# A norm's bias made with one streamed input, and a side factor loaded earlier into another home

## Chip, cores and metric

The kernel runs on one core of a Trainium2 chip. The metric is the device time of one execution in microseconds (us), the median of three. The engines are TensorE (PE in the rows; PEld is its weight load), VectorE (DVE), ScalarE (ACT), GpSimd (POOL) and SyncE (SP; SPq is its queue, which issues all DMAs). They run their own instruction streams in order and meet at semaphores.

## The reference

Two transformer layers with sandwich norms over x of 2 x 512 tokens and 512 channels. Each of four parts has, in short, the form

```python
x = x + _layernorm(part(_layernorm(x, axis=-1), ...), axis=-1)
```

with `part` = causal grouped attention with rotary embedding (32 heads, 8 key heads); a linear layer with a side branch; full attention with normed queries and keys (32 heads); a gated feed-forward layer with side branches. The linear part is

```python
h = jnp.einsum('bsd,nrd->nbsr', x, lora_A)
coef = (SCALE * lora_weights)[:, None, None]
lora_out = jnp.einsum('nbsr,nor->bso', h, lora_B * coef)
base = jnp.einsum('bsd,od->bso', x, W) + bias
return base + lora_out
```

and the norm is (x - m) / sqrt(v + eps) over the last axis, for each token.

## The kernel before

A tile is 128 tokens (8 tiles, 4 to a batch). Products are made of three fp32r matmuls (L83 to L85), with each operand split into `hi` and `lo`: ScalarE copies `hi`, VectorE or GpSimd subtracts (`rest`, L90) to get `lo`.

**The norm of rows** (class RowNorms) takes one tile at a time over three engines. VectorE makes statistics (L133), mean and variance (L139) and variance plus eps (L142). GpSimd takes the root (`root`, L148: the power -0.5 into `rstd`). VectorE makes the bias -mean*rstd (`center`, L154), and ScalarE applies scale and bias to the tile (`scaled`, L160). Every `[128, 1]` value of this is one column of a small tensor. The names are `first_norm` (8 tiles, before the first attention), `lin_norm` (4 rounds of 8: attention's output, linear input, linear output, next input) and `ffn_norm` (3 rounds of 8): 64 biases in all.

**The opening** runs the first norm over the 8 tiles. In each round VectorE centers tile t, then makes `xT_lo` of tile t-2 (L90). GpSimd's stream has, from tile 3 on, one split of a weight (L90, `l_w_k_lo` and `l_w_q_lo`) behind each root. TensorE turns the tiles and puts the first key and query projections between them.

**The first attention** runs 8 passes (one per key head) of 32 steps. What an engine does at a step is fixed by tables (`USES0`, `OUTS0`, `LOADS0`, `FETCH0`). Softmax rows are turned by VectorE (L1543) into `l_blocks`, moved between partitions by 16 DMAs for each pair of heads (L1236, `l_moved<-l_blocks`), and the sum over keys (`pv`) is scaled by VectorE (L1494, `l_scaled`). A pair's move waits until the buffer's earlier pair has gone through L1494.

**The last pass** goes on past step 32 and overlaps with the linear part (class Linear), whose constants are steps of that pass. The side factors are merged into the weight: `la` (factor a) and `lb` (factor b times mix times 2) are split, TensorE multiplies them at step 34 and 36 (MERGE), VectorE adds the product to the weight (L987), ScalarE and GpSimd split that. The loads are SP's: `load_a` at 12 into `l_raw_k`, `load_w` at 22 into `l_raw_q`, `load_b` at 28 into `l_raw_v`, which also issues the 1 MB load of `x` into `l_rope`. Since `l_raw_v` lies on the low half of the value weight, `load_b` waits for the last value projection. At SIDE (31) VectorE multiplies factor b by the mix (L976). From step 39 on, the norms of the linear part run, one or two tiles a step. GpSimd adds residuals there (L1050 `add`, L1053 `add_out`) behind its roots.

**The feed-forward phase** begins with the norms of 8 tiles in the same way (L2009 is its residual addition on GpSimd), while weights are merged and split.

Of the kernel before, what the change touches and what calls it, by code (L numbers as in the profile page):

```python
# [17 lines left out]
ALU = mybir.AluOpType  # L18
ACT = mybir.ActivationFunctionType
# [68 lines left out]
def rest(engine, out, full, hi):  # L88

    return engine.tensor_tensor(out, full, hi.bitcast(F32), ALU.subtract)  # L90
# [27 lines left out]
class RowNorms:  # L118
# [32 lines left out]
    def center(self, dve, r, t):  # L151

        dve.wait_ge(self.rooted[r], t + 1)
        dve.scalar_tensor_tensor(self.bias[:, r, t:t + 1], self.mean_var[:, r, t, 0:1], -1.0,  # L154
                                 self.rstd[:, r, t:t + 1], ALU.mult, ALU.mult).then_inc(self.biased[r], 1)

# [641 lines left out]
class Linear:  # L798
# [8 lines left out]
    FIRST = [(GH - 1) * TB + TB * GH * b + OUT0_AT + 1 for b in range(B)]  # L807
    LOAD_A, LOAD_W, LOAD_B, LOAD_LATE, SIDE, MERGE = 12, 22, 28, 33, 31, 34
    END = FIRST[1] + TB + AT[1]["split_next"]

    def __init__(self, p, ctx, ctx0, home, banks, xT, acc, ident, half, x_rows, kept):
        sem = lambda n: p.sem(ctx0, f"lin_{n}")
        self.p, self.nc, self.a = p, p.nc, p.a
        self.xT, self.acc, self.ident, self.x_rows, self.kept = xT, acc, ident, x_rows, kept
        self.w, self.la, self.lb, self.w_words, self.a_words, self.b_words, self.z, self.rope, self.blocks, self.bias = home
        self.z_next = self.rope[:, 2]
        self.x_first = self.rope[:, 0:2].rearrange("p a b s -> p (a b) s")
        self.x = [self.x_first[:, t] for t in range(TB)]
        self.x_second = self.blocks[:, 0].rearrange("p g c e i -> p (g c e i)")[:, 0:TB * D]            .rearrange("p (t d) -> p t d", t=TB)
        self.x += [self.x_second[:, t] for t in range(TB)]  # L820
        self.mix = p.sb(ctx, "lin_mix", [8 * RK, 1])
        self.score, self.general, self.out_bank, self.spare, self.brief = banks
        self.norms = RowNorms(p, ctx, ctx0, "lin_norm", 4, half)
        self.s_x = [sem("x_in0"), sem("x_in1")]
        self.s_a, self.s_b, self.s_w = sem("a_in"), sem("b_in"), sem("w_in")
        self.s_hi, self.s_lo, self.s_merged, self.s_whole, self.s_w_hi, self.s_w_lo, self.s_rows, self.s_taken = map(
            sem, "hi lo merged whole w_hi w_lo rows taken".split())
        self.s_add, self.s_add_out, self.s_turn, self.s_x_hi, self.s_x_lo = map(
            sem, "add add_out turn x_hi x_lo".split())
        self.s_turn_next, self.s_next_hi, self.s_next_lo, self.s_kept = map(  # L830
            sem, "turn_next next_hi next_lo kept".split())
# [27 lines left out]

    def load_a(self, sp):  # L860
        sp.dma_start(self.a_words[:], self.a["l0_a"]).then_inc(self.s_a, 16)

    def load_w(self, sp):
        sp.dma_start(self.w_words[:], self.a["l0_w"].rearrange("(c p) o -> p c o", p=P)).then_inc(self.s_w, 16)

    def load_b(self, sp):
        sp.dma_start(self.b_words[:], self.a["l0_b"]).then_inc(self.s_b, 16)
        sp.dma_start(self.x_first, self.x_rows[:, 0:TB]).then_inc(self.s_x[0], 16)
# [79 lines left out]
    def scalar(self, act, n):  # L948
# [4 lines left out]
        if n == self.SIDE + 1:  # L953
            act.wait_ge(self.s_lo, 1)
            act.activation(self.lb.hi, self.b_words[:], ACT.Copy).then_inc(self.s_hi, 1)
        for c in {self.MERGE + 2: (0, 1), self.MERGE + 4: (2, 3)}.get(n, ()):
# [16 lines left out]
    def vector_weights(self, dve, n):  # L973
        if n == self.SIDE:
            dve.wait_ge(self.s_b, 9 * 16)
            dve.tensor_scalar(self.b_words[:], self.b_words[:], self.mix[:], 2.0, ALU.mult, ALU.mult).then_inc(self.s_lo, 1)  # L976
        if n == self.SIDE + 1:
            dve.wait_ge(self.s_hi, 1)
            rest(dve, self.la.lo, self.a_words[:], self.la.hi).then_inc(self.s_lo, 1)
        if n == self.SIDE + 2:  # L980
            dve.wait_ge(self.s_hi, 2)
            rest(dve, self.lb.lo, self.b_words[:], self.lb.hi).then_inc(self.s_lo, 1)
        for c in {self.MERGE + 1: (0, 1), self.MERGE + 3: (2, 3)}.get(n, ()):
# [84 lines left out]
def grouped_attention(p, ctx0, xT, acc, ident, half, x_rows, kept, inv_rows):  # L1068
# [4 lines left out]
    with ExitStack() as ctx:  # L1073
# [79 lines left out]

        home = w_q, w_k[:], w_v[:], raw_q, raw_k, raw_v, trig, rope, blocks, mask
        last_pass = Pass(NG - 1, False, True, Linear.END)
# [36 lines left out]
        def _(sp):  # L1192
# [49 lines left out]
            def body(m):  # L1242
                for n in m.steps():
# [3 lines left out]
                    if pair is not None:  # L1247
                        move(m, pair)
                    if m.last and n == Linear.LOAD_A:
                        sp.wait_ge(s_bank, m.done(USES0, ("k", 1)))  # L1250
                        linear.load_a(sp)
                    if m.last and n == Linear.LOAD_W:
                        sp.wait_ge(s_bank, m.done(USES0, ("q", SLOTS - 1)))
                        linear.load_w(sp)
                    if m.last and n == Linear.LOAD_B:
                        sp.wait_ge(s_bank, m.done(USES0, ("v", 1)))
                        sp.nop(nofuse=True)
                        sp.wait_ge(s_rope_lo, m.done(USES0, ("q", SLOTS - 1), 0, of_qk))
                        linear.load_b(sp)
                    if m.last and n == Linear.LOAD_LATE:  # L1260
# [851 lines left out]
```

## Time and profile before

| | |
|---|---|
| median of 3 runs | 2323.69 us (2321.89 to 2324.77) |
| the profiled execution, its own time | 2323.8 us |
| its span | 2321.4 us |
| TensorE busy | 2112.8 us (91%) |
| VectorE busy | 1686.7 us (73%) |
| ScalarE busy | 1351.7 us (58%) |
| GpSimd busy | 1237.5 us (53%) |
| mean granted TensorE clock | 0.954 |

Busy time is the sum over an engine's instructions. The granted clock is 1.0 at 2.4 GHz and 0.5 at 1.2 GHz. The profiled execution lies 0.1 us from the median, so that a sum made against it holds for the median too.

### The profile page before, as it was taken

What the parts mean: (1) busy time and instruction counts of PE and PEld (TensorE: products, weight loads), DVE (VectorE), ACT (ScalarE), POOL (GpSimd) and SP (SyncE); (2) the same over time, 40 slices, a digit from 0 to 9 for tenths busy, and PEclk for the clock granted to TensorE, in tenths of its full rate; (3) what the DMA queues carried; (4) which work ended last, traced back from release to release, by engine and by line L of the source; (5) the groups of instructions that cost most, each with busy time, mean ns of one, the idle gap of its engine ahead of it and who ended that gap; (6) DMA issues with size and microseconds to landing.
All of it is one profiled execution on the core that took longest, in us unless ns stands there. A gap on an engine that the chain in (4) does not pass through costs nothing. (4 is left out here: it accounts for less than half of the span.)

```text
span 2321.4 us, 38455 instructions
## 1 busy us (share of the span) xinstructions
PE 2112.8 (91%) x10535; PEld 1781.2 (77%) x10535; DVE 1686.7 (73%) x2961; ACT 1351.7 (58%) x3637; POOL 1237.5 (53%) x996
## 2 busy tenths in 40 slices
PE   4899999999998745999999999999999999857998
PEld 3688888888886634888888888888888888635887
DVE  4788888888887772787878788787887888864422
ACT  4777777777776333665665656656656666433321
POOL 4878777787784434544545545455444454323400
PEclk8999999999999867999999999999999999977999
DMA  2344444434435111444444444344444443442210
GB/s 78 103 117 111 112 109 115 120 97 119 120 93 149 54 48 48 108 119 111 108 99 119 104 115 106 95 112 110 115 107 104 102 116 89 107 117 89 79 46 28
DMA packets 165903, 231.96 MB, mean 100 GB/s; under 512 B 47280, under 2 KB 77136, under 8 KB 165744
## 3 DMA queue, kind: packets, MB, share of 16 engines
q1 hardware_dynamic: 165744, 229.97, 37.1%
q8 instruction: 83, 1.36, 0.3%
q14 instruction: 76, 0.62, 0.1%
HBM read 114.23 MB, written 6.55 MB: 52 GB/s over the span
## 5 line engine op out<-in xcount | busy, mean ns | idle before, releaser
L90 POOL TENSOR_TENSOR l_probsT_lo<-l_moved,l_probsT_hi 128x512 fp32r<-128x512 f32 (+2 forms) x256 | 281.7, 1105 | 315.9 <-ACT l_probsT_hi L579 286.2
L573 ACT ACTIVATE l_probs<-l_score,l_negtop 128x512 f32<-128x512 f32 x256 | 175.7, 686 | 384.4 <-DVE l_negtop L675 384.1
L90 DVE TENSOR_TENSOR l_probsT_lo<-l_moved,l_probsT_hi 128x512 fp32r<-128x512 f32 (+1 forms) x256 | 284.4, 1111 | 30.5 <-ACT l_probsT_hi L579 30.4
L675 DVE TENSOR_REDUCE l_negtop<-l_score 128x1 f32<-128x512 f32 x256 | 175.8, 687 | 102.6 <-PE l_score L85 100.8
L1435 ACT ACTIVATE l_probs<-l_score,l_negtop 128x128 f32<-128x128 f32 (+3 forms) x256 | 134.8, 527 | 176.9 <-DVE l_negtop L1524 175.4
L83 PE MATMUL l_score<-l_kT_lo,l_qT_hi 128*128 128x512 f32 (+3 forms) x512 | 191.6, 374 | 50.4 <-POOL l_qT_lo L90 27.8
L83 PE MATMUL l_general<-l_w_qk_lo,xT_hi 128*128 128x512 f32 x512 | 201.1, 393 | 28.5 <-POOL l_w_qk_lo L90 28.5
L83 PE MATMUL l_out<-l_w_out_lo,l_oT_hi 128*128 128x512 f32 x512 | 209.6, 409 | 9.9 <-DVE l_oT_lo L90 7.2
L1524 DVE CUSTOM_DVE_ANT_0 l_score<-l_score,l_mask 128x128 f32<-128x128 f32 (+3 forms) x256 | 126.3, 493 | 112.5 <-PE l_score L85 111.7
L85 PE MATMUL l_out<-l_w_out_hi,l_oT_hi 128*128 128x512 f32 x512 | 201.8, 394 | 0.0
L84 PE MATMUL l_out<-l_w_out_hi,l_oT_lo 128*128 128x512 f32 x512 | 201.6, 394 | 0.0
L85 PE MATMUL l_general<-l_w_qk_hi,xT_hi 128*128 128x512 f32 x512 | 201.3, 393 | 0.0
L84 PE MATMUL l_general<-l_w_qk_hi,xT_lo 128*128 128x512 f32 x512 | 200.9, 392 | 0.0
L83 PE MATMUL l_general<-l_probsT_lo,l_v_hi 128*128 128x512 f32 (+3 forms) x512 | 183.3, 358 | 14.6 <-POOL l_probsT_lo L90 9.1
L85 PE MATMUL l_general<-l_probsT_hi,l_v_hi 128*128 128x512 f32 (+3 forms) x512 | 185.7, 363 | 0.0
L84 PE MATMUL l_general<-l_probsT_hi,l_v_lo 128*128 128x512 f32 (+3 forms) x512 | 185.1, 362 | 0.0
L84 PE MATMUL l_score<-l_kT_hi,l_qT_lo 128*128 128x512 f32 (+3 forms) x512 | 184.0, 359 | 0.0
L85 PE MATMUL l_score<-l_kT_hi,l_qT_hi 128*128 128x512 f32 (+3 forms) x512 | 183.8, 359 | 0.0
L690 DVE STREAM_TRANSPOSE l_blocks<-l_probs 128x512 f32<-128x512 f32 x256 | 177.9, 695 | 0.2 <-ACT l_probs L573 0.2
L90 POOL TENSOR_TENSOR l_w_qk_lo<-l_raw_qk,l_w_qk_hi 128x512 fp32r<-128x512 f32 x64 | 82.4, 1291 | 173.2 <-ACT l_w_qk_hi L543 173.2
L566 ACT ACTIVATE l_squares<-l_y 128x128 f32<-128x128 f32 x512 | 151.9, 299 | 28.7 <-DVE l_y L639 28.7
L83 PEld LDWEIGHTS l_score<-l_kT_lo,l_qT_hi 128*128 128x128 f32 x512 | 97.2, 190 | 77.6 <-ACT l_probs L1435 20.5
(215 smaller groups left out, 6391.6 us busy)
## 6 DMA issues: line engine op xcount, KB each, us to landing
l_moved<-l_blocks SPq DMA_DIRECT2D x1024, 64.0 KB, 2.0
l_moved<-l_blocks SPq DMA_DIRECT2D x512, 80.0 KB, 2.1
l_inv_all<-inv_rows SPq DMA_DIRECT2D x32, 512.0 KB, 4.3
l_raw_out<-l_wo SPq DMA_DIRECT2D x64, 256.0 KB, 4.4
l_inv_all<-inv_rows SPq DMA_DIRECT2D x64, 256.0 KB, 3.7
ffn_w_lo_words<-f_w SPq DMA_DIRECT2D x33, 256.0 KB, 2.8
l_raw_q<-l_wq SPq DMA_DIRECT2D x32, 256.0 KB, 4.2
l_raw_qk<-l_wq SPq DMA_DIRECT2D x64, 128.0 KB, 2.9
```

The lines of the kernel that those rows point to most:

```text
L83: nc.tensor.matmul(out, left.hi, right.lo, start=first, stop=False, skip_group_check=True)
L84: nc.tensor.matmul(out, left.lo, right.hi, start=False, stop=False, skip_group_check=True)
L85: return nc.tensor.matmul(out, left.hi, right.hi, start=False, stop=last, skip_group_check=True)
L90: return engine.tensor_tensor(out, full, hi.bitcast(F32), ALU.subtract)
L566: last = act.activation(squares[:, h], y[:, b, t, h * HD:(h + 1) * HD], ACT.Square, accum_out=sumsq[:, b, j:j + 1])
L573: act.activation(probs[:, n % NPR], score[n % 2][:], ACT.Exp, bias=negtop[:, n:n + 1], accum_out=total[:, n:n + 1]).then_inc(s_exp, 1)
L675: dve.tensor_reduce(negtop[:, n:n + 1], score[n % 2][:], AXX, ALU.max, negate=True)\
L690: dve.transpose(to, probs[:, n % NPR]).then_inc(s_block, 1)
L1435: act.activation(probs[:, n % NPR, 0:width[t]], score[n % 2][:, 0:width[t]], ACT.Exp, bias=negtop[:, n:n + 1], scale=-1.0, accum_out=total ...
L1524: dve.tensor_tensor_reduce(out=score[n % 2][:, 0:w], in0=score[n % 2][:, 0:w], in1=mask[:, S - w:S], scale=-SCALE, scalar=3.0e38, op0=ALU. ...
```

## The change

First, `center` makes the bias by `tensor_scalar` with the mean as its one streamed input and `rstd` as a per-partition scalar. Before, it was `scalar_tensor_tensor`, which streams both. Second, factor b is loaded with factor a at step 12 (of the pass; it was at 28) into the third place of `l_rope`, which the keys' rotation has left by then, and the multiplication, splits and copies of the side factors come one step sooner (SIDE is 30). The third place becomes `b_words`; `lb.lo` is no more made in place.

```diff
     def center(self, dve, r, t):
 
         dve.wait_ge(self.rooted[r], t + 1)
-        dve.scalar_tensor_tensor(self.bias[:, r, t:t + 1], self.mean_var[:, r, t, 0:1], -1.0,
-                                 self.rstd[:, r, t:t + 1], ALU.mult, ALU.mult).then_inc(self.biased[r], 1)
+        dve.tensor_scalar(self.bias[:, r, t:t + 1], self.mean_var[:, r, t, 0:1], self.rstd[:, r, t:t + 1], -1.0,
+                          ALU.mult, ALU.mult).then_inc(self.biased[r], 1)
...
-    LOAD_A, LOAD_W, LOAD_B, LOAD_LATE, SIDE, MERGE = 12, 22, 28, 33, 31, 34
+    LOAD_SIDE, LOAD_W, LOAD_X, LOAD_LATE, SIDE, MERGE = 12, 22, 28, 33, 30, 34
...
-        self.z_next = self.rope[:, 2]
+        self.z_next, self.b_words = self.rope[:, 2], self.rope[:, 2, 0]
...
-    def load_a(self, sp):
+    def load_side(self, sp):
         sp.dma_start(self.a_words[:], self.a["l0_a"]).then_inc(self.s_a, 16)
+        sp.dma_start(self.b_words, self.a["l0_b"]).then_inc(self.s_b, 16)
...
-    def load_b(self, sp):
-        sp.dma_start(self.b_words[:], self.a["l0_b"]).then_inc(self.s_b, 16)
+    def load_x(self, sp):
         sp.dma_start(self.x_first, self.x_rows[:, 0:TB]).then_inc(self.s_x[0], 16)
...
-                    if m.last and n == Linear.LOAD_A:
+                    if m.last and n == Linear.LOAD_SIDE:
                         sp.wait_ge(s_bank, m.done(USES0, ("k", 1)))
-                        linear.load_a(sp)
+                        sp.nop(nofuse=True)
+                        sp.wait_ge(s_rope_lo, m.done(USES0, ("k", 1), 0, of_qk))
+                        linear.load_side(sp)
...
-                    if m.last and n == Linear.LOAD_B:
-                        sp.wait_ge(s_bank, m.done(USES0, ("v", 1)))
-                        sp.nop(nofuse=True)
+                    if m.last and n == Linear.LOAD_X:
                         sp.wait_ge(s_rope_lo, m.done(USES0, ("q", SLOTS - 1), 0, of_qk))
-                        linear.load_b(sp)
+                        linear.load_x(sp)
```

On VectorE, at steps 30 to 33 of the last pass (L976 is the multiplication of factor b, L1524 the row minimum of step 31, `l_w_k_lo` and `l_w_v_lo` the low halves of `la` and `lb`), the order moves like this:

```order
 L90 TENSOR_TENSOR l_probsT_lo<-l_moved,l_probsT_hi 128x4x64
-L1524 ISA l_score,l_negtop<-l_score,l_mask 128x512
-L1524 ISA l_negtop 128x1
-L90 TENSOR_TENSOR l_v_lo<-l_general,l_v_hi 128x512
-L1543 STREAM_TRANSPOSE l_blocks<-l_probs 128x3x4x32
-L976 TENSOR_SCALAR l_raw_v<-l_raw_v,lin_mix 128x512
+L976 TENSOR_SCALAR l_rope<-l_rope,lin_mix 128x512
+L1524 ISA l_score,l_negtop<-l_score,l_mask 128x512
+L1524 ISA l_negtop 128x1
+L90 TENSOR_TENSOR l_v_lo<-l_general,l_v_hi 128x512
+L1543 STREAM_TRANSPOSE l_blocks<-l_probs 128x3x4x32
+L90 TENSOR_TENSOR l_w_k_lo<-l_raw_k,l_w_k_hi 128x512
```

The multiplication now stands ahead of step 31's row minimum, and `l_w_k_lo` ahead of the reciprocal and the last transposition. Nothing else on VectorE changes its place; each of the 64 biases keeps its row and changes its operation.

On SP, in the last pass (`l_raw_k<-l_a` is factor a, `l_rope<-l_b` factor b), two loads stand together:

```order
 L1239 DMA l_inv_all<-inv_rows 128x1024
 L861 DMA l_raw_k<-l_a 128x512
+L862 DMA l_rope<-l_b 128x512
 L1207 DMA l_raw_out<-l_wo 128x512
 L1227 DMA inv_rows<-l_inv 128x8
```

Factor b's 256 KB now go out between factor a's and a part of the output weight; behind step 28 the load of `x` follows the output weight directly.

## Rows read from the trace of the kernel before

**Rows 1.** Busy time by stretch: length, PE, PEld, DVE, ACT, POOL, PEclk, DMA share, GB/s.

```profile
742.40:759.20 16.80, 8.68 (x23) 6.36 (x22) 11.01 (x14) 5.88 (x13) 7.46 (x6) 0.59 0.54 159
787.60:792.60 5.00, 5.00 (x15) 4.00 (x14) 1.89 (x3) 0.64 (x2) 0.00 (x0) 0.52 0.00 0
```

**Rows 2.** Waits of TensorE between 716 and 2110 us: total, times, longest.

```profile
PE l_out L83 <- DVE l_oT_lo L90: 7.2, 2, 6.5
PE l_score L902 <- DVE xT_lo L90: 3.4, 1, 3.4
...
PE l_out L918 <- ACT l_rope L160: 9.1, 2, 7.3
...
PE ffn_rows L1798 <- ACT ffn_w_hi_words L160: 14.1, 3, 5.9
```

**Rows 3.** Instructions of single lines, ns min/median/max: L154, L142, L646, L976.

```profile
L154 DVE SCALAR_TENSOR_TENSOR lin_norm_bias<-lin_norm_mean_var,lin_norm_rstd x32: 146/647/1248, 765.4 to 862.5; 128x1 f32<-128x1 f32 x32
L154 DVE SCALAR_TENSOR_TENSOR ffn_norm_bias<-ffn_norm_mean_var,ffn_norm_rstd x24: 149/159/1214, 2067.3 to 2317.0; 128x1 f32<-128x1 f32 x24
L154 DVE SCALAR_TENSOR_TENSOR first_norm_bias<-first_norm_mean_var,first_norm_rstd x8: 159/1208/1225, 9.2 to 34.7; 128x1 f32<-128x1 f32 x8
...
L142 DVE TENSOR_SCALAR lin_norm_var<-lin_norm_mean_var x32: 133/153/156, 764.6 to 861.7; 128x1 f32<-128x1 f32 x32
...
L646 DVE SCALAR_TENSOR_TENSOR l_kT_lo<-l_general,l_gains,l_kT_hi x64: 750/751/754, 912.6 to 2013.0; 128x512 fp32r<-128x512 f32 x64
...
L976 DVE TENSOR_SCALAR l_raw_v<-l_raw_v,lin_mix x1: 486/486/486, 747.1 to 747.1; 128x512 f32<-128x512 f32 x1
```

**Rows 4.** Order of time, opening: start us, length us, engine, line, operation.

```profile
15.27 1.26 POOL L90 TENSOR_TENSOR l_w_k_lo<-l_raw_k,l_w_k_hi 128x512 fp32r<-128x512 f32 x1
15.34 1.21 DVE L154 SCALAR_TENSOR_TENSOR first_norm_bias<-first_norm_mean_var,first_norm_rstd 128x1 f32<-128x1 f32 x1 [0.66 <-POOL first_norm_rstd L148]
...
24.24 0.80 PE L83 MATMUL l_general<-xT_lo,l_w_k_hi 128*128 128x512 f32 x1 [2.13 <-DVE xT_lo L90]
```

**Rows 5.** Order of time, second attention and feed-forward phase.

```profile
1182.17 1.31 POOL L90 TENSOR_TENSOR l_w_qk_lo<-l_raw_qk,l_w_qk_hi 128x512 fp32r<-128x512 f32 x1
1182.63 0.75 DVE L646 SCALAR_TENSOR_TENSOR l_kT_lo<-l_general,l_gains,l_kT_hi 128x512 fp32r<-128x512 f32 x1 [0.28 <-ACT l_kT_hi L555]
...
2108.56 1.27 POOL L2009 TENSOR_TENSOR ffn_w_lo_words<-ffn_w_lo_words,acc 128x512 f32<-128x512 f32 x1 [0.67 <-ACT acc L160]
...
2108.94 0.15 DVE L142 TENSOR_SCALAR ffn_norm_var<-ffn_norm_mean_var 128x1 f32<-128x1 f32 x1
```

**Rows 6.** Groups of VectorE by shape: busy us, mean ns, idle before.

```profile
L90 DVE TENSOR_TENSOR l_qT_lo<-l_general,l_qT_hi 128x512 fp32r<-128x512 f32 x64 | 43.9, 686 | 7.4 <-ACT l_qT_hi L553 3.3
```

**Rows 7.** Busy time of L154 alone by stretch: length, DVE busy (x), PEclk, DMA, GB/s.

```profile
14.00:40.00 26.00, 6.08 (x5) 0.96 0.05 15
762.00:787.00 25.00, 5.35 (x8) 0.83 0.25 86
800.00:812.00 12.00, 3.12 (x4) 1.00 0.00 1
812.00:835.00 23.00, 7.32 (x11) 0.52 0.12 46
835.00:866.00 31.00, 5.65 (x9) 0.72 0.09 34
2070.00:2092.00 22.00, 4.01 (x6) 0.50 0.57 181
```

**Rows 8.** Order of time, last pass of the first attention.

```profile
738.69 1.53 POOL L90 TENSOR_TENSOR l_w_out_lo<-l_raw_out,l_w_out_hi 128x512 fp32r<-128x512 f32 x1 [2.13 <-ACT l_w_out_hi L1381]
...
741.82 0.37 SPq L867 DMA_DIRECT2D l_raw_v<-l_b  x1
...
747.14 0.49 DVE L976 TENSOR_SCALAR l_raw_v<-l_raw_v,lin_mix 128x512 f32<-128x512 f32 x1 [6.38 <-DMA l_raw_v<-l_b]
...
753.11 3.06 SPq L1236 DMA_DIRECT2D l_moved<-l_blocks  x5
```

More of the change, by code:

```diff
@@ L814, in __init__ @@
         self.xT, self.acc, self.ident, self.x_rows, self.kept = xT, acc, ident, x_rows, kept
-        self.w, self.la, self.lb, self.w_words, self.a_words, self.b_words, self.z, self.rope, self.blocks, self.bias = home
-        self.z_next = self.rope[:, 2]
+        self.w, self.la, self.lb, self.w_words, self.a_words, self.z, self.rope, self.blocks, self.bias = home
+        self.z_next, self.b_words = self.rope[:, 2], self.rope[:, 2, 0]
         self.x_first = self.rope[:, 0:2].rearrange("p a b s -> p (a b) s")
@@ L954, in scalar @@
             act.wait_ge(self.s_lo, 1)
-            act.activation(self.lb.hi, self.b_words[:], ACT.Copy).then_inc(self.s_hi, 1)
+            act.activation(self.lb.hi, self.b_words, ACT.Copy).then_inc(self.s_hi, 1)
         for c in {self.MERGE + 2: (0, 1), self.MERGE + 4: (2, 3)}.get(n, ()):
@@ L975, in vector_weights @@
             dve.wait_ge(self.s_b, 9 * 16)
-            dve.tensor_scalar(self.b_words[:], self.b_words[:], self.mix[:], 2.0, ALU.mult, ALU.mult).then_inc(self.s_lo, 1)
+            dve.tensor_scalar(self.b_words, self.b_words, self.mix[:], 2.0, ALU.mult, ALU.mult).then_inc(self.s_lo, 1)
         if n == self.SIDE + 1:
@@ L981, in vector_weights @@
             dve.wait_ge(self.s_hi, 2)
-            rest(dve, self.lb.lo, self.b_words[:], self.lb.hi).then_inc(self.s_lo, 1)
+            rest(dve, self.lb.lo, self.b_words, self.lb.hi).then_inc(self.s_lo, 1)
         for c in {self.MERGE + 1: (0, 1), self.MERGE + 3: (2, 3)}.get(n, ()):
@@ L1152, in bank_of @@
             return general[(m.number(USES0, x, d) - 1) % len(general)]
-        home = w_q, w_k[:], w_v[:], raw_q, raw_k, raw_v, trig, rope, blocks, mask
+        home = w_q, w_k[:], w_v[:], raw_q, raw_k, trig, rope, blocks, mask
         last_pass = Pass(NG - 1, False, True, Linear.END)
```

## The prediction

> **What bounds the kernel now.** I began with busy time by engine: TensorE is busy 91% of the span, so for most of the kernel nothing done to VectorE counts. What matters is where TensorE stands still, so next I read its waits by stretch [rows 2]. They lie in the opening, in the end of the last pass with the linear part (742 to 866 us), and at the head of the feed-forward phase (2070 to 2110 us). Nearly all end with VectorE or with ScalarE's norm step: 6.5 us on `l_oT_lo`, 3.4 on `xT_lo`, 9.1 on `l_rope` of L160, 14.1 on `ffn_w_hi_words` of L160. Those are the places where the biases are made. Third, I read the bias's own rows [rows 3]. A `[128,1]` result should cost 0.15 us, and the shortest do. But the median is 0.65 us in `lin_norm` and 1.21 us in `first_norm`, and the longest 1.25 us. In order of time one sees why [rows 4]: at 15.27 GpSimd begins a subtraction of 1.26 us with two SBUF inputs; at 15.34 the bias begins, and it lasts until 16.55, as GpSimd ends at 16.53. All long ones stand so beside a GpSimd operation that began just before them. It is no chance: GpSimd goes from the root straight to its next work, and VectorE starts the bias 0.07 us after. Fourth, the stall in the last pass [rows 8]: VectorE idles 6.38 us for factor b, issued at 741.82 with 1 MB of `x` behind it, and TensorE's 6.5 us are that stall.
>
> **Part 1: the bias.** Two things must hold, and the trace of before has both apart. Does an instruction with one streamed SBUF input and a per-partition scalar wait for GpSimd? L646 has such operands (its other stream is in PSUM). It runs 64 times in 750 to 754 ns [rows 3], although GpSimd is in the middle of an operation in some, as at 1182.63 [rows 5]: no wait. Does a `tensor_scalar` of `[128,1]` wait? L142 has this operation and shape, and takes 0.13 to 0.16 us 32 times in `lin_norm` [rows 3], and 0.15 at 2108.94 inside a GpSimd operation of 1.27 us [rows 5]. So I take the new bias as never held. Neither row has operation, shape and pointer scalar together, which leaves the rival below. The scalar has a price: L646 takes 751 ns, and a subtraction of the same size from PSUM without a scalar 686 [rows 6]. So 0.065 us an instruction; the bounds are 0 and 0.065.
>
> The Trainium skill speaks against this part too. "SBUF — State Buffer", section Who interferes with whom, says that a VectorE instruction with two SBUF inputs contends with a GpSimd instruction that reads SBUF (the trace agrees: 1.21 against 0.16 us), but also that `tensor_scalar` can enter a two-port mode in which the second to issue fully blocks. By that the new bias would be held as the old one; L142's rows are against it at this shape.
>
> What is held is the busy time of L154 less 0.155 us for each instruction [rows 7]:
> - Opening: 5 held, 6.08 - 0.78 = 5.3. Only the first three (tiles 3 to 5) lie ahead of the first projection, which waits for `xT_lo` of tile 3 at 24.24 [rows 4]; TensorE is then busy past the other two. 3 x 1.06 = **3.2 us**.
> - 762 to 787: 5.35 - 8 x 0.155 = **4.1**. VectorE hardly idles there, and TensorE waits for it (3.4 on `xT_lo`).
> - 800 to 835: 3.12 + 7.32 - 14 x 0.155 (one lies on the border) = **8.3**. Here each tile is a chain of statistics, root, bias, scaling.
> - 835 to 866: 5.65 - 9 x 0.155 = **4.3**.
> - 2070 to 2092: 4.01 - 6 x 0.155 = **3.1**, three held, each ahead of an L160 on which TensorE waits.
>
> In the two middle stretches VectorE also takes TensorE's results, which can't come sooner at two places; my estimate for this is 0.6 off. Behind a bias come statistics (one SBUF input, not held), so GpSimd's operation is over before VectorE has two inputs again; I expect little of the hold to come back. GpSimd, busy 53% of the span, has a root or two and one addition for each tile, while VectorE and ScalarE have more, so it doesn't become the bound. Sum 23.0 - 0.6 = 22.4. Some 36 new biases lie on the path: 36 x 0.065 = 2.3 lost. The other instructions of the kernel's 64 are covered by TensorE.
>
> With less idle time ahead of the first linear products, TensorE may keep its clock. From 787.6 to 792.6 it was granted 0.52, the 1.2 GHz level [rows 1], after a wait of 3.4 us. More than half of the 4.1 us of holds ahead lie inside or just before this wait, so it shrinks to 1 us or so. At the upper level these 5.0 us take half: 2.5. Bounds 0 and 2.5; I take 2.0.
>
> **Part 2: the load.** The new order puts L976 (0.49 us) ahead of step 31's row minimum, at about 739.0, with its data there since shortly after step 12. Nothing waits for the load itself. SP gets one more wait, on the last key's rotation at step 8, four steps past; behind it stand only loads with slack, and 256 KB cost them some 0.4 us. At 739.0 GpSimd is in `l_w_out_lo` (738.69 to 740.22, [rows 8]). L976 takes 0.95 ns a column, the fastest of VectorE's rows, so it may use both of its ports and be held: 0 or 1.2 us; I take 1.2. So the stall of 6.4 turns into 1.2 of hold: 5.2 saved on VectorE. Its 0.49 us are only moved.
>
> What is late next? The stall also holds L1494 of the third head pair's buffer and with it the last move, whose first DMA goes at 753.11 [rows 8]; this comes about 6 us sooner and still takes 10 us of SP's issuing (16 DMAs at 3.06 / 5 us), which starts to bound ScalarE's copies of step 40 (they then wait for the landing, not for VectorE). TensorE, on the other side, gains more than the stall: from 742.4 to 759.2 it is busy 8.68 of 16.8 us at 0.59 of the clock [rows 1]; at the upper level the same work takes about 5.2, which gives back up to 3.5. VectorE's 11.0 us in the same stretch cap it. So 5.2 at least and 6.4 + 3.5 = 9.9 at most; by following each step past 746 I get 8, since the moved chain lets VectorE reach step 41 some 8 us sooner. I take **8.0**.
>
> **The sum.** 22.4 - 2.3 + 2.0 + 8.0 = 30.1. The profiled execution's own time is 2323.8 (its span of 2321.4 and 2.4 around it), and the median of the runs 2323.69, so nothing is shifted between them: 2293.7, say **2294 us** (1.3% less).
>
> **Rivals.**
> - *The bias is held as before* (a two-port mode, or the scalar read through the shared port). Only part 2 remains, less the scalar's 2.3: 2323.8 - 8 + 2 = 2318; L142 and L646 speak against it. 6%.
> - *The gain comes back along the linear part.* Moves (10 us of issue) or TensorE's products set the end of each stretch, and of the 16.7 us of holds there only about a third counts. 2323.8 - 8 - 3.2 - 3.1 - 5.6 + 2.3 = 2306. For it speaks that TensorE has long runs of products between the waits; against it, that it waits 3.4 and 9.1 us for this very chain. 10%.
> - *The stall stays and only the biases gain* (the side factor's chain waits for something else at step 30, such as ScalarE's copies): 2323.8 - 22.1 = 2302. The rows name the DMA as releaser and nothing else. 2%.
> - *Slower.* The per-partition form has a high fixed cost at `[128,1]`, which L142 doesn't show because its scalar is an immediate. It decides above (22.4 + 8 + 2) / 36 = 0.9 us more for each bias, in all 36 places on the path; at 1.1 us more the time is 2331. L646 and L976 (486 ns in all, with a pointer scalar) put it near 0.065. 2%.
> - The forecast: 80%.
>
> **How the numbers follow.** With part 2 at 5.2, no clock gain and 85% of the holds, the forecast's case gives 2323.8 - 5.2 - 19.0 + 2.3 = 2302; with 9.9, 2.5, all 23.0 and no price for the scalar it gives 2288. The rival of the third line lies in it. I take 2286 to 2303, which leaves some 2 in 10 outside. A measurement of this kernel tells about 0.2% (4.6 us) from no change. Faster holds in all cases but the slow one: 97%; within 0.2% 1%, slower 2%.
>
> **What would show it.** L154 at 0.20 to 0.23 us 64 times, none above 0.3; if a part of them is 1.2, the first rival. The first projection at 21.1 to 21.3 instead of 24.24. L976 behind `l_probsT_lo` without a DMA as releaser, and 1.2 us longer if held. TensorE's 6.5 us wait down to about 2, the last move's first DMA some 9 us sooner with the opening's 3.2 in it. The last `xT_lo` of the linear part about 27 us sooner than 866. The clock at the first linear products near 1.0; if it is 0.5, 2 us are missing. Wrong would make me: holds that go over to the next VectorE instruction with two inputs, waits of ScalarE on the moves in place of the stall, or a linear part that TensorE bounds.

## The result

The changed kernel takes 2297.23 us (median of 4 runs, 2295.63 to 2299.46) and the kernel before 2323.77 (4 runs beside them, 2321.89 to 2324.77): a ratio of 0.9887, 95% interval 0.987 to 0.9905, 26.5 us less. The prediction was 2294 us, with 2286 to 2303 as its range. The profiled execution has a span of 2293.8 us, 27.6 less than that of before.

The page of the profile after; the two rows of busy time are its engines and the granted clock in 40 slices:

```profile
span 2293.8 us, 38455 instructions
PE 2107.2 (92%) x10535; PEld 1778.1 (78%) x10535; DVE 1666.9 (73%) x2961; ACT 1350.7 (59%) x3637; POOL 1237.4 (54%) x996
PEclk8999999999999968999999999999999999977999
```

The lines L154 and L976 after (ns min/median/max), which answer to [rows 3]:

```profile
L154 DVE TENSOR_SCALAR lin_norm_bias<-lin_norm_mean_var,lin_norm_rstd x32: 198/213/216, 756.6 to 837.0; 128x1 f32<-128x1 f32 x32
L154 DVE TENSOR_SCALAR ffn_norm_bias<-ffn_norm_mean_var,ffn_norm_rstd x24: 203/214/215, 2042.8 to 2289.3; 128x1 f32<-128x1 f32 x24
L154 DVE TENSOR_SCALAR first_norm_bias<-first_norm_mean_var,first_norm_rstd x8: 213/214/215, 9.3 to 32.9; 128x1 f32<-128x1 f32 x8
...
L976 DVE TENSOR_SCALAR l_rope<-l_rope,lin_mix x1: 1520/1520/1520, 737.9 to 737.9; 128x512 f32<-128x512 f32 x1
```

None of the 64 biases is held (the longest takes 216 ns). The price is that the usual one takes 213 ns, where the short ones of before took 149 to 159: 0.06 us for the scalar. L976 has no DMA ahead of it any more, and is now held itself. In order of time one sees by what (changed kernel, end of the last pass; start, length, engine):

```profile
737.59 1.53 POOL L90 TENSOR_TENSOR l_w_out_lo<-l_raw_out,l_w_out_hi 128x512 fp32r<-128x512 f32 x1 [2.13 <-ACT l_w_out_hi L1381]
...
737.88 1.52 DVE L976 TENSOR_SCALAR l_rope<-l_rope,lin_mix 128x512 f32<-128x512 f32 x1
...
746.11 4.31 SPq L1236 DMA_DIRECT2D l_moved<-l_blocks  x7
```

GpSimd began 0.29 us before, and VectorE ends 0.28 us after it: 1.03 us of hold. The last move's first DMA goes at 746.11, 7.0 us sooner than in [rows 8]. TensorE's waits after, between 716 and 2082 us, which answer to [rows 2]:

```profile
PE ffn_rows L1798 <- ACT ffn_w_hi_words L160: 12.3, 3, 5.9
...
PE l_out L918 <- ACT l_rope L160: 5.4, 2, 4.8
...
PE l_out L83 <- DVE l_oT_lo L90: 3.2, 2, 1.7
...
PE l_score L902 <- DVE xT_lo L90: 2.0, 1, 2.0
```

The 6.5 us of the stall are 1.7, the wait ahead of the first linear products went from 3.4 to 2.0, and the two on `l_rope` of L160 from 9.1 to 5.4. The stretches that answer to [rows 1] (length, PE, PEld, DVE, ACT, POOL, PEclk):

```profile
740.00:749.00 9.00, 6.06 (x29) 4.39 (x28) 9.00 (x15) 6.52 (x14) 4.01 (x4) 1.00 0.77 242
749.00:757.00 8.00, 7.91 (x42) 6.58 (x40) 7.28 (x13) 2.54 (x6) 7.55 (x7) 1.00 0.54 125
765.00:772.00 7.00, 6.97 (x24) 6.01 (x25) 4.49 (x14) 3.88 (x7) 5.78 (x6) 0.56 0.00 0
776.00:781.00 5.00, 5.00 (x28) 4.38 (x27) 3.61 (x7) 0.94 (x2) 0.00 (x1) 1.00 0.00 0
```

Around the former stall the clock is 1.00 (it was 0.59), and the first linear products run at the upper level (1.00, it was 0.52); 765 to 772 is mostly at the lower one (0.56).

**Where the time came from.** I take the same instruction in both traces and subtract its starts:

| instruction | before | after | shift | this stretch | predicted, net |
|---|---|---|---|---|---|
| first key projection (L83) | 24.24 | 21.49 | -2.75 | | |
| last move's inverse load before the stall | 740.64 | 739.54 | -1.1 | -1.1 | -3.0 |
| first statistics of `lin_norm` (L133) | 763.66 | 754.28 | -9.38 | -8.3 | -8.0 |
| 8th statistics of `lin_norm` | 783.64 | 772.33 | -11.31 | -1.9 | -3.6 |
| first L1023 | 792.88 | 779.10 | -13.78 | -2.5 | -2.0 |
| L1023 of tile 4 | 841.04 | 819.18 | -21.86 | -8.1 | -7.1 |
| last statistics of `lin_norm` | 860.79 | 835.28 | -25.51 | -3.65 | -3.4 |
| first L139 of `ffn_norm` | 2064.01 | 2039.48 | -24.53 | +1.0 | 0 |
| L139 at the head of the phase's products | 2108.72 | 2081.17 | -27.55 | -3.0 | -2.7 |

The last column is the prediction's term with the scalar's price (0.065 for each bias there) and its 0.6 taken off (0.3 in each of the two stretches from 800 to 866). It sums to 29.8 and not to the 30.1 on record, because these stretches hold 40 biases (3, 8, 14, 9 and 6) and the prediction took the price for "some 36". Two terms are clearly too large: the opening and the stretch to 783.

### The profile page after: what moved, and what is told of

Same layout as the page of the kernel before. It is cut to its first block and busy times, and to the rows that moved or that the text cites. A ratio compares the mean times of both kernels' runs of the same rounds, so it can differ in the third digit from the quotient of the medians.

```text
span 2293.8 us, 38455 instructions
## 1 busy us (share of the span) xinstructions
PE 2107.2 (92%) x10535; PEld 1778.1 (78%) x10535; DVE 1666.9 (73%) x2961; ACT 1350.7 (59%) x3637; POOL 1237.4 (54%) x996
## 3 DMA queue, kind: packets, MB, share of 16 engines
q8 instruction: 83, 1.36, 0.3%
## 5 line engine op out<-in xcount | busy, mean ns | idle before, releaser
L90 POOL TENSOR_TENSOR l_probsT_lo<-l_moved,l_probsT_hi 128x512 fp32r<-128x512 f32 (+2 forms) x256 | 282.0, 1106 | 313.6 <-ACT l_probsT_hi L579 286.7
L90 DVE TENSOR_TENSOR l_probsT_lo<-l_moved,l_probsT_hi 128x512 fp32r<-128x512 f32 (+1 forms) x256 | 285.9, 1117 | 30.5 <-ACT l_probsT_hi L579 30.5
L83 PE MATMUL l_score<-l_kT_lo,l_qT_hi 128*128 128x512 f32 (+3 forms) x512 | 191.2, 373 | 50.4 <-POOL l_qT_lo L90 28.9
L83 PE MATMUL l_general<-l_w_qk_lo,xT_hi 128*128 128x512 f32 x512 | 201.6, 394 | 28.5 <-POOL l_w_qk_lo L90 28.5
L83 PE MATMUL l_out<-l_w_out_lo,l_oT_hi 128*128 128x512 f32 x512 | 209.3, 409 | 6.0 <-DVE l_oT_lo L90 3.2
L1524 DVE CUSTOM_DVE_ANT_0 l_score<-l_score,l_mask 128x128 f32<-128x128 f32 (+3 forms) x256 | 126.2, 493 | 113.1 <-PE l_score L85 112.0
L83 PE MATMUL l_general<-l_probsT_lo,l_v_hi 128*128 128x512 f32 (+3 forms) x512 | 183.3, 358 | 14.5 <-POOL l_probsT_lo L90 10.2
L90 POOL TENSOR_TENSOR l_w_qk_lo<-l_raw_qk,l_w_qk_hi 128x512 fp32r<-128x512 f32 x64 | 82.4, 1291 | 173.3 <-ACT l_w_qk_hi L543 173.3
L83 PEld LDWEIGHTS l_score<-l_kT_lo,l_qT_hi 128*128 128x128 f32 x512 | 97.2, 190 | 77.6 <-ACT l_probs L1435 20.5
```

The lines of the kernel that those rows point to most:

```text
L83: nc.tensor.matmul(out, left.hi, right.lo, start=first, stop=False, skip_group_check=True)
L1524: dve.tensor_tensor_reduce(out=score[n % 2][:, 0:w], in0=score[n % 2][:, 0:w], in1=mask[:, S - w:S], scale=-SCALE, scalar=3.0e38, op0=ALU. ...
```

## The experiments

Each is timed against the kernel before, run beside it. That kernel's median went from 2320 to 2325 us between batches of runs, so I give ratios; 0.001 is 2.3 us.

**1. The parts alone.** `bias_only` is the kernel before with the new `center`; `load_only` is the changed kernel with the old one:

```diff
 load_only
-        dve.tensor_scalar(self.bias[:, r, t:t + 1], self.mean_var[:, r, t, 0:1], self.rstd[:, r, t:t + 1], -1.0,
-                          ALU.mult, ALU.mult).then_inc(self.biased[r], 1)
+        dve.scalar_tensor_tensor(self.bias[:, r, t:t + 1], self.mean_var[:, r, t, 0:1], -1.0,
+                                 self.rstd[:, r, t:t + 1], ALU.mult, ALU.mult).then_inc(self.biased[r], 1)
```

> The kernel before with the new bias alone (load and side factors as before). If the prediction's terms stand: 22.4 of holds, 2.0 of clock, less 2.3 for the scalar, so 22.1 less than before: 2301.6 us. If the terms have the sizes that the changed kernel's trace shows (opening 1.1, 762 to 787 about 2, clock 2.5, then 7.5, 3.7 and 3.0): 19.8 less, 2304. If the clock at the first linear products was the load's doing and not the bias's: 2306.5, with TensorE's products there at the lower level. If the two parts share a gain (one bounds what the other gives), this and load_only together save clearly more or less than 26.5.

> The changed kernel with the old bias instruction. Theory: the load is worth what the shift in the trace shows at 760 us, 8.3 less, so 2315.4 us, and L154 is as long as before (median 0.65 us in lin_norm, some 1.2). Rival 1: only the stall itself less the hold counts, 5.2: 2318.5. Rival 2: the clock at the first linear products comes with the load, 8.3 + 2.5: 2313. In all of them L976 is held for 1.5 us, as in the changed kernel.

Measured: `bias_only` 0.992 (0.9903 to 0.9936), 18.6 us less, between the 19.8 and the 17.3 of its second and third case; `load_only` 0.9968 (0.9956 to 0.9979), 7.4 less, near the 8.3 of its theory. Together 26.0, beside the 26.5 of both at once: the parts add up within what can be told. By the shifts of the same instructions, the linear part of `load_only` begins 8.2 us sooner (its first L133 stands at 756.52, 7.14 sooner, behind an opening that is 1.0 later), and its last statistics are 8.25 sooner; in `bias_only` the first are 0.2 sooner and the last 16.9 (860.79 against 843.90).

In two stretches the parts show what the sum hides. From the first to the eighth statistics (763.66 to 783.64 before) `bias_only` gains 2.6 us, `load_only` loses 0.45, and both together gain the 1.9 of the table, where 3.6 was predicted: most of what is missing there is missing with the bias alone. And from the eighth statistics to the first L1023 the time is 9.24 us before, 8.36 in `bias_only`, 8.27 in `load_only` and 6.77 in the changed kernel. In each part alone the first linear products still run in part at the lower clock (a granted 0.66 and 0.74 over the first 5 us, 0.52 before), but it rises earlier than before, and that gives 0.9 and 1.0 us; only both at once give the 2.5.

**2. What is held.** `ports` is a kernel of its own, in the order of a norm; it copies `x` to the output and leaves out the rest of the work:

```python
# GpSimd, each round
pool.tensor_tensor(rstd[:, 0:1], var[:], half[:], ALU.pow).then_inc(s_root, 1)
pool.tensor_tensor(lo[:], full[:], hi[:], ALU.subtract).then_inc(s_rest, 1)
# VectorE, each round
dve.wait_ge(s_root, k + 1)
form(dve, f, w, beside[f]).then_inc(s_done, 1)
dve.wait_ge(s_rest, k + 1)
dve.wait_ge(s_done, 2 * k + 1)
form(dve, f, w, alone[f]).then_inc(s_done, 1)
```

> A kernel of its own that copies x to the output and computes nothing of the reference. In each round GpSimd makes a [128,1] power, then at once a [128,512] subtraction of two SBUF tensors; VectorE waits for the power and issues one instruction of a given form beside the subtraction, and the same form again with GpSimd idle (tiles named beside and alone). Seventeen forms, six times each. Theory: two SBUF streams are held whatever the width (stt_1, tt_1 about 1.2 us beside and 0.15 alone), one stream of [128,1] with a scalar from SBUF isn't (0.21 both), one stream of [128,512] is (ts_512 about 1.5 beside, 0.49 alone), as L976. A form with one of its streams in PSUM isn't held, nor is bn_stats. The rival for L976: it is not its width, but that GpSimd's instruction had begun before, or its in-place write; then ts_512 is 0.49 in both. Open, and read from the run: from which width on (2, 4, 16, 64, 128) one stream is held, and whether a stride of two elements takes the hold away.

Its groups by shape (busy us, mean ns, idle before); `ts` is `tensor_scalar` with a scalar from SBUF, `stt` `scalar_tensor_tensor`, and `apart` reads every second element:

```profile
L144 DVE SCALAR_TENSOR_TENSOR stt_beside<-left,right 128x1 f32<-128x1 f32 x6 | 7.1, 1190 | 5.9 <-POOL rstd L176 5.9
...
L144 DVE SCALAR_TENSOR_TENSOR stt_alone<-left,right 128x1 f32<-128x1 f32 x6 | 1.0, 159 | 0.6
...
L142 DVE SCALAR_TENSOR_TENSOR stt_psum_beside<-bank,right 128x1 f32<-128x1 f32 x6 | 0.9, 158 | 4.0 <-POOL rstd L176 4.0
...
L156 DVE TENSOR_SCALAR ts_beside<-left,scale 128x1 f32<-128x1 f32 x6 | 1.3, 214 | 4.0 <-POOL rstd L176 4.0
...
L156 DVE TENSOR_SCALAR ts_alone<-left,scale 128x1 f32<-128x1 f32 x6 | 1.3, 214 | 6.1 <-POOL lo L177 6.1
...
L156 DVE TENSOR_SCALAR ts_beside<-left,scale 128x2 f32<-128x2 f32 x6 | 7.3, 1218 | 4.0 <-POOL rstd L176 4.0
...
L156 DVE TENSOR_SCALAR ts_alone<-left,scale 128x2 f32<-128x2 f32 x6 | 1.4, 228 | 0.6
...
L156 DVE TENSOR_SCALAR ts_beside<-left,scale 128x512 f32<-128x512 f32 x6 | 8.9, 1477 | 4.0 <-POOL rstd L176 4.0
...
L156 DVE TENSOR_SCALAR ts_alone<-left,scale 128x512 f32<-128x512 f32 x6 | 2.9, 486 | 0.6
...
L155 DVE TENSOR_SCALAR ts_apart_beside<-left,scale 128x64 f32<-128x64 f32 x6 | 7.5, 1242 | 4.0 <-POOL rstd L176 4.0
```

One stream of one column is never held (214 ns beside and alone), of two columns it is (1218 against 228), and so with 4, 16, 64, 128 and 512 (odd widths above one weren't run). A source read with a stride of two is held too. Two SBUF streams are held at one column already (1190 against 159), and with one of them in PSUM not at all (158; at 512 columns 691 and 692). `bn_stats` isn't held (695 in both). The Trainium skill, "VectorE: DVE Perf Modes", section What auto-detection actually checks, lets an instruction with a single source take the two-port mode when source and destination are in SBUF and their outermost non-unit dimensions are both even or equal. A `[128,1]` operand has no such dimension, and if that keeps it out of the mode, the run agrees: no hold at one column, a hold at every even width tried. The mode itself is in no row, but the rates fit: alone, the one-stream form grows by 0.52 ns a column (254 ns at 64 columns, 486 at 512), and the two-stream form by 1.04 (159 at one, 693 at 512). For a width of one this answers the doubt that the prediction took from "SBUF — State Buffer".

**3. Two columns in the kernel.** The same bias, with one column more; the bias tile gets two columns for each value, and ScalarE reads the first:

```diff
-        dve.tensor_scalar(self.bias[:, r, t:t + 1], self.mean_var[:, r, t, 0:1], self.rstd[:, r, t:t + 1], -1.0,
+        dve.tensor_scalar(self.bias[:, r, t], self.mean_var[:, r, t], self.rstd[:, r, t:t + 1], -1.0,
                           ALU.mult, ALU.mult).then_inc(self.biased[r], 1)
```

> The changed kernel with the bias instruction made two columns wide (it scales mean and variance together; the second column is read by nobody). Nothing else differs. By the ports run, one stream of two columns is held and of one isn't; so the 64 instructions are held where the old ones were, 1.2 us where GpSimd has begun, and the time goes to about that of load_only, 2316 us (2297.2 + 18). Rival: the hold went with the second stream and width has nothing to do with it in the kernel: 0.23 us each and 2298 us.

Measured: 0.998 (0.9969 to 0.999), against 0.9887 of the changed kernel: some 21 us given back for one column, about the whole gain of `bias_only`. Its L154 (the ones of `lin_norm` go up to 1253 ns):

```profile
L154 DVE TENSOR_SCALAR first_norm_bias<-first_norm_mean_var,first_norm_rstd x8: 227/1218/1233, 9.3 to 35.3; 128x2 f32<-128x2 f32 x8
```

**4. The price of a column instruction.** Each bias is made twice:

```diff
+        for end in (False, True):
+            made = dve.tensor_scalar(self.bias[:, r, t:t + 1] if end else self.spare[:, r, t:t + 1],
+                                     self.mean_var[:, r, t, 0:1], self.rstd[:, r, t:t + 1], -1.0, ALU.mult, ALU.mult)
...
```

> The changed kernel with each of the 64 biases made twice, the first time into a column that nobody reads. It measures what one more column instruction costs where the biases stand. If 36 of them are on the path, as the prediction counted, and one takes 0.15 to 0.21 us of VectorE: 5.4 to 7.6 slower than the changed kernel, 2303 to 2305 us. If only a third of them is on the path: about 2.5 slower, 2300. If the two overlap on VectorE so that the second is nearly free: below 2, 2298 to 2299.

Measured: 0.9896 (0.9879 to 0.9912), 2 us more than the changed kernel, with intervals that overlap, and less than the 5.4 to 7.6 expected for 36 biases on the path. In the trace two such instructions start 0.12 to 0.13 us apart, so 36 on the path would be 4.5 us. In the linear part the shift against the changed kernel goes from -1.2 to +2.8 us, 4.0 for 32 biases, of which 1.7 fall between the eighth statistics and the first L1023, mostly on the clock. With that piece the count of the prediction fits (4.0 / 0.125 is 32, where it had 31 in this part); without it some 18 are left. So the price of one more column instruction on the path is 0.12, the scalar's share of it 0.06 by experiment 2, and how many are on the path stays open between a half and all of the prediction's count.

**5. The opening.** `warm` adds work for TensorE ahead of the key projection (`WARM` is {1: 2, 2: 2, 3: 4, 4: 6}):

```diff
                 last.then_inc(s_out, 1)
+                if t in WARM:
+                    for k in range(WARM[t]):
+                        pe.transpose(score[0][:, k % 4 * P:(k % 4 + 1) * P], ident[:], ident[:])
```

> The changed kernel with 14 more transpositions of the identity on TensorE in the opening (2, 2, 4 and 6 behind those of tiles 1 to 4) into a score bank that nobody uses yet; nothing waits for them but TensorE itself. Theory: the opening gave 1.1 to 1.3 and not 3.2 because TensorE, which starts the key projection 2.75 us sooner, does all 12 products of it at the lower clock (5.28 us against 4.49). With TensorE busier before, the clock rises sooner: the projection takes 3 to 4.5 us, the first score comes 1 to 2 us sooner than 44.92, and the time is 2295 to 2296. Rival: the second row minimum and all behind it are bound by something else (VectorE, the loads), so the first score moves and 51.59 doesn't: 2297. Second rival: the clock doesn't answer to this work, and the products start later: 2297 to 2298.

In the changed kernel the key projection begins sooner, but its 12 matmuls start 0.43 us apart to the end (0.59 behind the first), the lower level; it takes 5.28 us to the transpositions at 26.77. Before, the last four were 0.23 apart, and it took 4.49 (24.24 to 28.73). The first projection of the changed kernel and the end of the same piece:

```profile
21.49 0.80 PE L83 MATMUL l_general<-xT_lo,l_w_k_hi 128*128 128x512 f32 x1 [1.13 <-DVE xT_lo L90]
...
26.35 0.63 PE L85 MATMUL l_general<-xT_hi,l_w_k_hi 128*128 128x512 f32 x1
26.77 0.76 PE L1321 MATMUL l_out<-ident,l_probs 128*128 128x128 f32 x4
```

And in `warm`:

```profile
21.41 0.80 PE L83 MATMUL l_general<-xT_lo,l_w_k_hi 128*128 128x512 f32 x1
22.01 0.63 PE L84 MATMUL l_general<-xT_hi,l_w_k_lo 128*128 128x512 f32 x1
22.43 0.51 PE L85 MATMUL l_general<-xT_hi,l_w_k_hi 128*128 128x512 f32 x1
22.78 0.39 PE L83 MATMUL l_general<-xT_lo,l_w_k_hi 128*128 128x512 f32 x1
...
24.86 0.60 PE L1324 MATMUL l_out<-ident,l_probs 128*128 128x128 f32 x4
```

3.45 us for the same 12 matmuls, and the second score product comes 3.1 us sooner than in the changed kernel (47.76 against 50.85). So the theory of the opening holds: with the clock up, the opening gives what was missing. The time doesn't follow: 0.9955 (0.9938 to 0.9973), some 16 us worse than the changed kernel by ratios. The profile is of the fastest of six executions (2301.5 us, the median is 2308.1), so it shows only a part of this loss: 6.9 us between 888 and 2039 us. Experiment 7 is about that.

**6. The hold of L976, and GpSimd's own bias.** `mix_sooner` moves the multiplication alone, `gpsimd_bias` takes the bias from VectorE:

```diff
 mix_sooner
-        if n == self.SIDE:
+        if n == self.SIDE - 1:
             dve.wait_ge(self.s_b, 9 * 16)
 gpsimd_bias, in root, behind the power
+        pool.wait_ge(self.rooted[r], t + 1)
+        pool.tensor_scalar(self.bias[:, r, t:t + 1], self.mean_var[:, r, t, 0:1], self.rstd[:, r, t:t + 1], -1.0,
+                           ALU.mult, ALU.mult).then_inc(self.biased[r], 1)
```

> The changed kernel with the mix multiplication (L976) alone one step sooner, ahead of step 30's row minimum, where VectorE idles 1.5 us behind l_probsT_lo. Theory: its 1.52 us (0.49 of work, 1.03 of hold by GpSimd's l_w_out_lo) lie on VectorE's path at step 31, and in the idle time they cost nothing, held or not: the first statistics of lin_norm come 1.5 us sooner than 754.28 and the time is 2295.7. Rival: VectorE's chain there is bound by the moves' landing (ScalarE waited 4.4 us for one at 758.16), so nothing or 0.5 is left: 2297.

> The changed kernel with the bias made by GpSimd itself, right behind the root, and none on VectorE. VectorE loses 0.125 us a bias and its waits for the root (0.62, 0.66, 0.44 and 1.40 between 756 and 773, where it bounds), up to 4 us; GpSimd gets one more [128,1] instruction behind each root, an estimate of 0.2 to 0.5 us, and each scaling by ScalarE comes that much later. Where each tile is one chain (812 to 866, and six at the head of the feed-forward phase) that costs 20 to 25 times the difference to VectorE's 0.2. If the waits weigh more: 2294 to 2296. If the chains weigh more: 2299 to 2303.

`mix_sooner`: 0.9911 (0.9895 to 0.9928), no gain; by ratios it is 5.6 us slower than the changed kernel, with intervals that overlap. Its first statistics come 4.6 us sooner than in the changed kernel (1.7 of it from an opening in which the clock rose earlier), the first linear product is still 2.2 ahead (773.91 against 776.07), and by 785 it is 0.2 behind. TensorE's transposition ahead of the first linear products, and their stretch, show why (`mix_sooner`):

```profile
773.17 1.09 PE L902 MATMUL l_score<-ident,l_trig 128*128 128x128 f32 x4 [3.53 <-DVE xT_lo L90]
```

```profile
774.00:778.00 4.00, 4.00 (x12) 3.13 (x11) 1.74 (x3) 0.60 (x1) 0.00 (x0) 0.50 0.00 0
```

It waited 3.53 us there (2.01 in the changed kernel) and then worked at a granted clock of 0.50. From the eighth statistics to the first L1023 it takes 9.51 us, where the changed kernel takes 6.77. So the theory's local part was right and its time wrong: of the 4.6 us, 2.1 went to waits up to the eighth statistics (the first bias alone waits 1.98 for its root, where it waited 0.62), and TensorE's clock took back the other 2.5.

`gpsimd_bias`: 0.9874 (0.9858 to 0.9891), the better of the two cases expected. GpSimd's bias takes 0.27 us and begins 0.10 behind the root, and VectorE neither makes it nor waits for the root:

```profile
L151 POOL TENSOR_SCALAR lin_norm_bias<-lin_norm_mean_var,lin_norm_rstd 128x1 f32<-128x1 f32 x32 | 8.5, 264 | 3.2
```

The same kernel again, this time beside the changed one:

> The changed kernel once more, beside the runs below. It asks two things. Is the ratio to the kernel before again 0.987 to 0.9905? And does TensorE start the first linear products at the upper clock again, as in the first profile (9 us of products in 3.0)? In bias_only, load_only, warm, mix_sooner and gpsimd_bias they began at the lower one, though the stall was gone in four of them; if so here too, the clock term of 2.5 us is chance of the execution; if not, it hangs on the exact times of this kernel.

> The kernel with GpSimd's own bias once more, now on the chip that runs the changed kernel too. In the first run its ratio to the kernel before was 0.9874 (0.9858 to 0.9891), in the profile its linear part ended 3.3 us sooner than the changed kernel's and its span was 3.5 less. If that is real, it is 3 to 7 us faster than after_again (2290 to 2294 us). If the gain was the chip's, both are within 2 us.

`after_again` 2299.57 us, 0.9892 (0.9874 to 0.9909); `gpsimd_again` 2294.62 us, 0.9874 (0.9857 to 0.989). Their intervals overlap, but in both batches the ratio is 0.9874, and in both profiles the last statistics of its linear part come 2.5 to 3.2 us sooner (832.11 and 832.82 against 835.28 and 835.35). It is the fastest version tried, by an estimated 3 to 5 us. The changed kernel's second profile repeats the first one's to 0.2 us up to 888 us, clock at the first linear products included, so the clock there repeats with the kernel's exact times, as far as two profiles tell, and isn't chance of an execution. From there to 2039 us it loses 4.1 us.

**7. TensorE without work in the second attention.**

> As warm, with 16 more transpositions in place of 14 (3, 3, 4 and 6). The opening was 3.2 us better in warm, yet the time 9 to 11 us worse; in its profile TensorE stands twice in each hardware-loop pass of the second attention with nothing that it waits for (1.4 to 1.9 us at the first score, and again 1.5 to 1.8 at a value projection 3 us later), where the changed kernel stands once. Theory: what counts is where the loop's instructions lie, which 28 more instructions ahead of it (14 loads of a weight, 14 products) have moved, so another number gives another count of stands: with 16, either once in each pass and a time of 2294 to 2296, or twice and 2302 to 2308. Rival: the second stand comes from the clock or another cause in the opening's work, so it is there with any number of them; then 2302 to 2308 for this one and a loss for gpsimd_warm_8 too.

> GpSimd's own bias, and 8 more transpositions in the opening (4 behind those of tiles 3 and 4). If the place of the loop's instructions decides and 8 leaves TensorE with one stand in each pass: 1 to 3 us faster than gpsimd_again, by the key projection at the upper clock (3.5 us instead of 4.9 or more). If it stands twice in each pass: 5 to 9 us slower than gpsimd_again.

Measured: `warm_16` 0.996 (0.9947 to 0.9972), a median of 2314.6 us and so slower than both cases expected; `gpsimd_warm_8` 0.9881 (0.9863 to 0.9898), 1.6 us slower than `gpsimd_again` by ratio and 4.1 by medians, between its two cases. A stand is here a time in which TensorE idles while it waits for nothing that the profile shows. The rows of TensorE's waits between 880 and 2040 us that end with "issue" (total, times, longest), of the changed kernel:

```profile
PE l_score L83 <- issue: 8.7, 5, 2.1
...
PE l_general L85 <- issue: 0.8, 1, 0.8
```

of `warm`:

```profile
PE l_general L83 <- issue: 8.0, 5, 1.8
PE l_score L83 <- issue: 7.8, 5, 1.9
```

of `warm_16`:

```profile
PE l_general L84 <- issue: 12.5, 5, 3.1
PE l_score L83 <- issue: 10.6, 5, 2.2
```

and of `gpsimd_warm_8`:

```profile
PE l_score L83 <- issue: 10.6, 5, 2.3
PE l_general L83 <- issue: 4.3, 3, 2.1
```

Each kernel stands five times at a score, some 142 us apart; the second attention's hardware loop has six passes, so five returns to its start. Those with added instructions stand a second time, 3 to 4 us later, in three to five of the passes. Without added instructions a second stand is rare and short: 0.8 us in all here, none in `after_again` and `load_only`, 1.0 in `gpsimd_again`, 1.8 in `mix_sooner`. The number of added instructions changes the place, the length and the count of the second stands, and the work added is far away in time. In `warm_16` one sees what a stand costs besides itself:

```profile
1306.81 0.49 PE L83 MATMUL l_score<-l_kT_lo,l_qT_hi 128*128 128x512 f32 x1 [2.13 <-issue]
...
1310.41 0.37 PE L84 MATMUL l_general<-l_w_v_hi,xT_lo 128*128 128x256 f32 x1 [2.43 <-issue]
1310.58 0.42 PE L85 MATMUL l_general<-l_w_v_hi,xT_hi 128*128 128x256 f32 x1
1310.80 0.41 PE L83 MATMUL l_general<-l_w_v_lo,xT_hi 128*128 128x256 f32 x1
```

Behind the second stand its matmuls start 0.21 us apart until 1314.4 and 0.12 apart from there on: a granted clock of 0.50 from 1310.5 to 1314.4, and 1.00 from 1314.5. Twelve and a half us of stands and five such stretches, some 2 us each by my estimate, account for the 20 us that `warm_16` loses to the changed kernel between 888 and 2039 us.

That the code's place decides the stands is the theory that fits (three numbers of added instructions, three patterns), and the DMA packets speak for it. The trace has packets of 16 KB of the kind "instruction" on a queue q8. Within a pass of the changed kernel they go out 15 to 27 us apart, but around each score stand four go within 12 us (at 1158.4, 1160.2, 1163.6 and 1168.3, for instance). One ends 1.5 to 1.9 us ahead of the end of each of the five score stands, in both profiles of the changed kernel, and one ends 1.3 to 1.4 ahead of the end of each second stand of `warm_16`. So TensorE's stands go together with the loading of code at the loop's returns. That it waits for this code is still argued, not shown: no row says which engine the queue serves, and no run moved the loop and nothing else.

## Why the prediction was right, and where it was off

- **"I take the new bias as never held": right**, 64 of 64, and experiments 2 and 3 show the reason to be narrower than the prediction had it. It isn't one stream, it is one stream and one column. L142 was the row that told it, and L646 was no evidence for a `tensor_scalar`: one of its streams is in PSUM, and that form isn't held at 512 columns (691 ns), where `tensor_scalar` is.
- **The scalar's 0.065: right** (0.06; L154 213 ns against 153 of L142).
- **Part 2, 8.0 us: right**, 8.3 in the table and 8.2 in `load_only`. Of its pieces, the hold of L976 was 1.03 (1.2 predicted), the clock around the former stall 1.00, the last move 7.0 sooner with 1.1 of opening in it, 5.9 where the text expected about 6.
- **The opening, 3.2 us: mis-sized, 1.1 measured.** VectorE's part came (the first projection 2.75 sooner), and TensorE, asked sooner, worked at the lower clock for longer: 0.8 us went in the key projection and 0.6 more by the second score (52.19 against 50.85). The prediction had costed the clock at the linear products and not here. How much stays also differs between kernels with the same opening: against the kernel before, the first scores of `load_only`, whose opening is unchanged, come 1.0 us later, and those of `mix_sooner`, whose opening is that of the changed kernel, 3.0 sooner against its 1.3.
- **762 to 787, 4.1 less the scalar's 0.5: mis-sized, 1.9.** The five long biases gave 3.9 us, and some 1.9 went to other places. The first bias had found its root ready, and now waits 0.62 for it; `l_probsT_lo` is held a little longer (1.36 us, 1.16 before); and one root comes late:

```profile
770.12 0.68 DVE L90 TENSOR_TENSOR l_probsT_lo<-l_moved,l_probsT_hi 128x512 fp32r<-128x512 f32 x1
770.16 1.49 POOL L90 TENSOR_TENSOR l_probsT_lo<-l_moved,l_probsT_hi 128x384 fp32r<-128x384 f32 x1
771.62 0.54 POOL L148 TENSOR_TENSOR lin_norm_rstd<-lin_norm_var,half 128x1 f32<-128x1 f32 x1
...
772.20 0.21 DVE L154 TENSOR_SCALAR lin_norm_bias<-lin_norm_mean_var,lin_norm_rstd 128x1 f32<-128x1 f32 x1 [1.40 <-POOL lin_norm_rstd L148]
```

  VectorE's subtraction begins 0.04 us ahead of GpSimd's here, and GpSimd's takes 1.49 us; before, GpSimd's began 0.98 ahead (781.21 against 782.19) and took 1.00. The root comes behind it, and the bias waits 1.40 where it had waited 0.44: 1.0 us. The prediction had named "holds that go over" as what would make it wrong, but to the next VectorE instruction with two inputs, which is only 0.2 us here; the larger part went over to GpSimd. `bias_only` has the late root too (a wait of 1.41) and gains 2.6 us, so this part comes with the new bias; the first bias's wait comes with the load (`load_only` has it, 0.62, and `bias_only` doesn't).
- **The clock, +2.0: right in size (2.5), and luckier than its reason.** The wait ahead shrank to 2.0 us and not to 1, and the lower clock went to 765 to 772, where VectorE bounds anyway. In `bias_only` and `load_only` the same term was 0.9 and 1.0, and in `mix_sooner` the stretch took 0.3 more than before. About half of it would have been its fair price.
- **800 to 866, 12.6 before deductions, and 2070 to 2092, 3.1: right**, 11.7 and 3.0 measured against 10.5 and 2.7 net of deductions.
- **A wait that the prediction passes over.** TensorE's longest wait in this span is neither VectorE's nor ScalarE's: 19.09 us for GpSimd's `l_w_qk_lo` (L90), up to 883.87, between the linear part and the second attention (19.2 after). It follows the linear part as a whole, so the gain passes through it: L646 first stands at 912.60 before and 887.60 after, 25.0 sooner. The prediction's "nearly all end with VectorE or with ScalarE's norm step" leaves it out, and that did no harm here.
- **Rivals.** "Held as before" is excluded by every L154; `two_columns` is what it would have looked like. "The gain comes back along the linear part" happened to 1.7 us of 16.7, in the first of its three stretches. "Slower" would have needed 0.9 us a bias, and it is 0.06.

## What to carry to other kernels

Look at the median, not the best, of small VectorE instructions beside GpSimd's; a `[128,1]` value that takes 0.2 us alone and 1.2 beside GpSimd is cured by having one streamed input and one column, or one of two streams in PSUM. Price a sooner start of TensorE by what its clock will be there: a gain that leaves TensorE waiting in another place can be taken back whole, as in `mix_sooner`. And when a change adds instructions to an engine whose stream has a hardware loop, look at the "issue" waits of the loop's passes before blaming the change.

## What was not expected of the hardware

- One column or two decide over 1.0 us: 214 against 1218 ns beside the same GpSimd subtraction.
- With fourteen transpositions added in the first 21 us, TensorE's second stands between 1160 and 1760 us sum to 8.0 us, with sixteen to 12.5 and with eight (and GpSimd's bias) to 4.3; without any they were 0 to 1.8.
- Two profiles of one kernel agree to 0.2 us up to 888 us, and then part by 4.1 us in the second attention, where the stands at the scores sum to 8.7 us in one and 9.9 in the other. At 1449 us TensorE stood 1.40 us in the first and 2.04 in the second, and from 1450 to 1470 the granted clock was 1.00 and 0.91. Most of the spread between runs may come from there; that is an estimate from two profiles.
